# Weight preparation of a recurrent layer: staged W_ih loads, row sums of absolute values on ScalarE, low parts as identity products on TensorE

## The chip, the cores and the metric

One NeuronCore of a Trainium2 chip runs the whole program. The metric is the device time of one execution in microseconds (us). Engine names as in the profile: PE is TensorE (PEld its weight loads), DVE VectorE, ACT ScalarE, POOL GpSimd, SP the engine that only issues transfers here. Each engine works through its own instructions strictly in order. They wait for each other by semaphores.

## The reference

Inputs: x (16 sequences, 256 steps, 512 features) and cond_2048 (16 x 512). Two layers follow each other, each added to its input:

1. Layer 0. Eight block sums of each sequence are scored, weighted and projected to one vector per sequence. It is added to x, and a layer norm follows. Then a feed-forward network (gate, up, down, 512 to 2048 to 512) whose activations and weights are all quantised in blocks of 32. x1 = x + the result.
2. Layer 1. A GRU over the 256 steps with cond_2048 as its first state: gi = x1 W_ih + b_ih and gh = h W_hh + b_hh (each 512 to 1536, cut in thirds r, z, n); r = sigmoid(i_r + h_r), z = sigmoid(i_z + h_z), n = tanh(i_n + r h_n), h' = (1 - z) n + z h. On the states a linear layer with a bias and a mixture of 16 low-rank experts, of which a small router picks two. The output is x1 + the result.

## The kernel before

**Tiles and slots.** The 4096 rows are cut into 32 tiles of 8 time steps times 16 sequences. `over_tiles` (L261) runs a loop of c = -3 to 32, and in each c eight slots s = 0 to 7. It is a software pipeline: at c, the norm and quantisation work on tile c + 4, gate and up on tile c + 3, down and x1 on tile c + 2, the products x1 W_ih on tile c + 1, the recurrence on tile c (one time step per slot, L1283 to L1287 for PE and `recur`, L712, for DVE), and the linear layer with experts on tile c - 1. So the recurrence starts at c = 0. Each engine has a function `slot(c, s)` that issues its instructions in an order written out by hand. There is no planner: an instruction that waits holds up everything behind it on its engine.

**Before the tiles.** `over_pieces` (L273) quantises the feed-forward weights in 24 pieces of 128 x 1024, each going through DVE, POOL, PE (transposes) and ACT (L416 keeps them). Attention and the norm of the first tile run beside the later pieces. c = -3 follows when the last piece is through: PE waits for all 24 kept pieces (L1299).

**High and low parts.** A product of the GRU has nearly fp32 accuracy because each weight and each state is scaled by a power of two and stored as two fp16 numbers, high = fp16(S w) and low = fp16(S w - high). The scale comes from the largest absolute value:

- c = -3, W_hh (loaded into `wih` chunks 0 to 3, each 128 x 1536 fp32). Slot 0: DVE reduces each chunk to a maximum per row (L672), and h as well (L677). PE turns the maxima into a row (`weights_scales`, s = 0, L1272). Slot 1: DVE computes the scales in one partition (`scales_in_row`, L614, L682, L685), and PE spreads them over the partitions (L1277). Slot 2: ACT keeps them (L445, L446). Slots 3 to 6: ACT writes the high part of chunk k (L451), DVE the low part (L699).
- c = -3, slot 6: SP issues the load of the linear layer's weights (`wl`, 1664 KB) and, as the low parts of W_hh are finished, the four chunks of W_ih (768 KB each) into chunks 1 to 4 of the same tile `wih` (L372, L373).
- c = -2, W_ih. Slot 0: DVE reduces its four chunks (L636) and `wl` (L641). Scales as above in slots 0 and 1 (L646 to L652). Slots 3 to 6: high part on ACT (L456), low part on DVE (L658). They are written into the chunk below, so that ACT waits for the low part before.
- c = -1: the first products x1 W_ih (L1151), which need x1T (ACT L502, DVE L903, both in slot 7 of c = -2).
- c = 0: the first state products (L1257) and the parts of `wl`.

**Around it in the same slots**, for the feed-forward tiles f = c + 3 and e = c + 2: PE gate (L1084) in even slots and up (L1090) in odd ones, ACT silu (L475) and DVE the product `inter` (L801) with its quantisation (L762 to L786), POOL qf (L979), PE transposes (L1099) that ACT keeps (L481), and down (L1108). For tile q = c + 4: DVE statistics (L878) and xn (L884, slot 2), POOL times gamma and plus beta (L989, L991). In `slot` of PE the scale products (`weights_scales`) stand ahead of the gate and up products.

Of the kernel before, what the change touches and what calls it, by code (L numbers as in the profile page):

```python
# [24 lines left out]
BF16 = mybir.dt.bfloat16  # L25
# [8 lines left out]
P = 128  # L34
# [28 lines left out]
FILLS = 6  # L63
# [26 lines left out]
def build(nc, x_steps, h0, ident, pick, block_mask, iota, rms_w, query, WkT, WoT, gamma, beta,  # L90
          ffn_w, W_ih, W_hh, b_ih, b_hh, WL, bias, rb1, rw2T, rb2, gates, BT, x1_dram, out):
    with ExitStack() as ctx:
        def sb(name, shape, dt=F32):
            return ctx.enter_context(nc.sbuf_tensor(name, shape, dt))
# [4 lines left out]
        def bank(name):  # L99
# [15 lines left out]
        wih, wl = sb("wih", [P, KD + 1, GATES]), sb("wl", [P, KD + 1, D + ROUTE])  # L115
# [3 lines left out]
        bt = sb("bt", [P, XA // P, D])  # L119
# [51 lines left out]
        x1_in, x1_bias, y = sb("x1_in", [P, D]), sb("x1_bias", [P, D]), sb("y", [P, D])  # L171
# [11 lines left out]
        wst = [sb("wst0", [P, PIECE]), sg_gs[:, 0:PIECE]]  # L183
        qfT_flat = qfT[:, :, :].rearrange("p k n -> p (k n)")
        wy = [gi[:, u * PIECE:(u + 1) * PIECE] for u in range(2)]
        wm = [gi[:, 2 * PIECE:3 * PIECE], sb("wm1", [P, PIECE])[:, :]]
# [18 lines left out]
        chunk_max, most = sb("chunk_max", [P, KD]), sb("most", [P, 2])  # L205
# [15 lines left out]
                             "wl_low_part"))  # L221
        x_small, x_row_ok, x_row_mm, x_scale_mm, x_scale_ok, x_hi = (
# [100 lines left out]
        def _(sp):  # L323
# [61 lines left out]
        def _(act):  # L385
# [54 lines left out]
            def weights(c, s):  # L440

                if c in (-3, -2) and s == 2:
# [5 lines left out]
                if c == -3 and 3 <= s < 3 + KD:  # L448
                    k = s - 3
# [88 lines left out]
        def _(dve):  # L538
# [91 lines left out]
            def input_weights(c, s):  # L630

                at = 2 * KD + 9
                if (c, s) == (-2, 0):
                    for k in range(KD):
                        dve.wait_ge(wih_loaded, 16 * KD)
                        v.tensor_reduce(chunk_max[:, k:k + 1], wih[:, k + 1, :], AX_X, ALU.max,  # L636
                                        apply_absolute_value=True).then_inc(most_dve, 1)
                    dve.wait_ge(most_dve, at)
                    v.reduce_max(most[:, 0:1], chunk_max[:, :], AX_X).then_inc(most_dve, 1)
                    dve.wait_ge(wl_loaded, 16)  # L640
                    v.tensor_reduce(most[:, 1:2], wl[:, 1:KD + 1, :].rearrange("p k n -> p (k n)"), AX_X, ALU.max,  # L641
                                    apply_absolute_value=True).then_inc(most_dve, 1)
# [11 lines left out]
                if c == -2 and 3 <= s < 3 + KD:  # L654
                    k = s - 3
                    dve.wait_ge(scale_kept, 2)
                    dve.wait_ge(wih_hi, k + 1)
                    v.scalar_tensor_tensor(wih_parts[:, k, GATES:2 * GATES], wih[:, k + 1, :], S_I,  # L658
                                           wih_parts[:, k, 0:GATES], ALU.mult, ALU.subtract).then_inc(wih_lo, 1)
# [6 lines left out]
            def gru_weights(s):  # L666


                if s == 0:
                    for k in range(KD):  # L670
                        dve.wait_ge(whh_loaded, 16 * KD)
                        v.tensor_reduce(chunk_max[:, k:k + 1], wih[:, k, :], AX_X, ALU.max,  # L672
                                        apply_absolute_value=True).then_inc(most_dve, 1)
                    dve.wait_ge(most_dve, KD)
                    v.reduce_max(most[:, 0:1], chunk_max[:, :], AX_X).then_inc(most_dve, 1)
# [3 lines left out]
                if s == 1:  # L679
                    dve.wait_ge(most_mm, 1)  # L680
                    scales_in_row(s, KD + 2, least, scale_row)
                    v.tensor_tensor(scale_row[:, 2:3], scale_row[:, 0:1], scale_row[:, 1:2],  # L682
                                    ALU.mult).then_inc(most_dve, 1)
                    dve.wait_ge(most_dve, KD + 8)
                    v.reciprocal(scale_row[:, 3:4], scale_row[:, 2:3]).then_inc(most_dve, 1)  # L685
                if s == 3:
# [9 lines left out]
                if s in (3, 4, 5, 6):  # L696
                    k = s - 3
                    dve.wait_ge(whh_hi, k + 1)
                    v.scalar_tensor_tensor(whh[:, k, 1, :], wih[:, k, :], S_W, whh[:, k, 0, :], ALU.mult,  # L699
                                           ALU.subtract).then_inc(whh_lo, 1)  # L700
# [205 lines left out]
            def slot(c, s):  # L906
# [13 lines left out]
                if c in (-2, 0):  # L920
                    input_weights(c, s)
# [10 lines left out]
        def _(pool):  # L932
            g = nc.gpsimd
            g.memset(minus_half[:, :], -0.5).then_inc(filled, 1)
            g.memset(least_l[:, :], LEAST).then_inc(filled, 1)
# [83 lines left out]
        def _(pe):  # L1019
# [243 lines left out]
            def weights_scales(c, s):  # L1263

                at = (c + 3) * (KD + 9)
                if s == 0:
                    pe.wait_ge(most_dve, at + KD + 2)
# [6 lines left out]
                if s == 1:  # L1274
                    pe.wait_ge(filled, FILLS)
                    pe.wait_ge(most_dve, KD + 9 if c == -3 else 2 * KD + 20)
                    mm(ps_route[:, 0:4], ones_row[:, :], (scale_row if c == -3 else scale_row_l)[:, :], start=True,  # L1277
                       stop=True).then_inc(scale_mm, 1)

            def slot(c, s):  # L1280
# [14 lines left out]
                others(c, s, Q, F, E, I, L)  # L1295

# [60 lines left out]
```

## Time and profile before

| | us |
|---|---|
| median of 3 executions | 1827.99 (1827.65 to 1829.74) |
| the profiled execution, its own time | 1829.66 |
| its span, first to last instruction | 1827.8 |
| PE busy | 1595.1 (87%) |
| DVE busy | 1512.8 (83%) |
| ACT busy | 662.1 (36%) |
| POOL busy | 512.6 (28%) |

The profile is of one execution. Its own time is 1.86 us above its span. Where below the granted clock of TensorE is given, 1.00 is 2.4 GHz and 0.50 is 1.2 GHz; between them both occurred in the stretch. A group of instructions that follow each other is printed as one row with its count. The last duration in a row of matmuls includes the drain of the array. An fp32 matmul of 128 x 512 appears as two records.

### The profile page before, as it was taken

The numbers are of one execution on the slowest core, as the hardware profiler recorded it, in microseconds if no ns is written. First come the engines' busy times: TensorE is split into PE (matmuls) and PEld (weight loads), VectorE is DVE, ScalarE is ACT, GpSimd is POOL, SyncE is SP. The second block draws the span as 40 slices with busy tenths as digits, with TensorE's granted clock in tenths as the row PEclk, the third lists the DMA queues.
The fourth block names the chain that finished last, engine by engine and source line by source line (L and its number), as shares of the span: only waits on it lengthen the run. The fifth ranks groups of instructions, "written<-read, shape, count | busy, mean of one in ns | idle before, by whom it ended". The sixth has DMA issues, their size and how long they took to land.

```text
span 1827.8 us, 76340 instructions
## 1 busy us (share of the span) xinstructions
PE 1595.1 (87%) x32908; PEld 1245.7 (68%) x32908; DVE 1512.8 (83%) x5651; ACT 662.1 (36%) x1712; POOL 512.6 (28%) x572
## 2 busy tenths in 40 slices
PE   5422247999999999999999999999999999999986
PEld 2211114787787778777777777877777777778874
DVE  8999988888888888888888888888888888887654
ACT  1111124444434343443434444344344444344331
POOL 4545423222222222222222222222222222221001
PEclk8755568999999999999999999999999999999997
DMA  6413120000101011000001000001010010000000
GB/s 246 169 63 133 55 92 30 26 15 32 32 32 32 32 32 32 32 32 32 27 31 32 32 32 32 32 32 32 31 32 32 32 32 32 27 19 23 31 15 19
DMA packets 35409, 80.10 MB, mean 44 GB/s; under 512 B 4864, under 2 KB 5248, under 8 KB 34688
## 3 DMA queue, kind: packets, MB, share of 16 engines
q1 hardware_dynamic: 28080, 63.09, 10.1%
q10 hardware_dynamic: 6992, 12.13, 1.9%
q8 instruction: 259, 4.24, 1.0%
q14 instruction: 78, 0.64, 0.1%
HBM read 58.43 MB, written 16.78 MB: 41 GB/s over the span
## 4 chain that ended last, share of the span: by engine, by line
PE 72%; DVE 23%; issue 3%; ACT 1%; DMA 1%; POOL 0%; DVEq 0%; ACTq 0%; SPq 0%; POOLq 0%
PE ps_rn L1257 22%; PE ps_gi L1151 11%; PE ps_z L1257 10%; PE ps_gate_up L1090 6%; PE ps_down L1108 6%; PE ps_base L1160 4%; PE ps_gate_up L1084 4%; PE ps_base L1204 3%; PE ps_route L1160 3%; DVE gi L570 2%; DVE gi L567 2%; DVE wam L544 1%; DVE gi L572 1%; DVE wm L567 1%; DVE fe L769 1%
## 5 line engine op out<-in xcount | busy, mean ns | idle before, releaser
L1257 PE MATMUL ps_rn<-hT,whh 128*128 128x32 f16 x16320 | 449.1, 176 | 37.3 <-DVE hT L707 37.1
L1257 PEld LDWEIGHTS ps_rn<-hT,whh 128*128 128x128 f16 x16320 | 434.9, 96 | 64.0 <-DVE hT L707 58.1
L979 POOL TENSOR_TENSOR qf<-f8c,fe 128x512 bf16<-128x512 bf16 x128 | 135.8, 1061 | 887.1 <-DVE f8c L786 867.6
L1151 PE MATMUL ps_gi<-x1T,wih 128*128 128x128 f16 x4608 | 288.6, 219 | 1.2 <-ACT gi L515 1.2
L1151 PEld LDWEIGHTS ps_gi<-x1T,wih 128*128 128x128 f16 x4608 | 270.3, 98 | 25.6 <-issue 1.5
L524 ACT ACTIVATE r_tanh<-r_pre,scale_half 128x64 f32<-128x64 f32 x256 | 89.0, 348 | 458.3 <-DVE r_pre L727 458.3
L1257 PE MATMUL ps_z<-hT,whh 128*128 128x32 f16 x8160 | 243.2, 176 | 0.0
L1257 PEld LDWEIGHTS ps_z<-hT,whh 128*128 128x128 f16 x8160 | 222.6, 96 | 0.0
L515 ACT ACTIVATE gi<-ps_gi,b_i,scale_x 128x128 f32<-128x128 f32 x384 | 144.7, 457 | 190.7 <-PE ps_gi L1151 190.7
L721 DVE TENSOR_TENSOR r_half<-ps_rn,gi 128x64 f32<-128x64 f32 x256 | 56.6, 221 | 135.4 <-PE ps_rn L1257 135.1
L1084 PE MATMUL ps_gate_up<-wq,qxT 128*128 128x512 bf16 x512 | 134.6, 385 | 14.2 <-DVE inter L801 14.2
L526 ACT ACTIVATE z_tanh<-z_pre,scale_half 128x64 f32<-128x64 f32 x256 | 89.0, 348 | 159.8 <-DVE z_pre L737 159.8
L1090 PE MATMUL ps_gate_up<-wq,qxT 128*128 128x512 bf16 x512 | 137.6, 393 | 2.4 <-ACT sg_gs L475 2.4
L1108 PE MATMUL ps_down<-wq,qfT 128*128 128x512 bf16 x512 | 135.3, 388 | 0.0
L1160 PE MATMUL ps_base<-wl,hT 128*128 128x512 f16 x384 | 96.3, 388 | 0.0
L528 ACT ACTIVATE n<-n_pre,scale_half 128x64 f32<-128x64 f32 x256 | 89.0, 348 | 16.0 <-DVE n_pre L744 5.9
L801 DVE TENSOR_TENSOR inter<-ps_gate_up,sg_gs 128x512 f32<-128x512 f32 x128 | 87.3, 682 | 6.2 <-PE ps_gate_up L1090 6.2
L762 DVE TENSOR_REDUCE fam<-inter 128x16 f32<-128x512 f32 x128 | 87.9, 686 | 4.4
L475 ACT ACTIVATE sg_gs<-ps_gate_up 128x512 f32<-128x512 f32 x128 | 74.2, 580 | 41.7 <-PE ps_gate_up L1084 41.7
L780 DVE SCALAR_TENSOR_TENSOR f<-inter,finv 128x512 fp8e4<-128x512 f32 x128 | 87.6, 684 | 0.0
L1108 PEld LDWEIGHTS ps_down<-wq,qfT 128*128 128x128 bf16 x512 | 48.8, 100 | 50.4 <-issue 5.5
L1090 PEld LDWEIGHTS ps_gate_up<-wq,qxT 128*128 128x128 bf16 x512 | 43.1, 99 | 54.5 <-issue 19.8
(201 smaller groups left out, 2663.6 us busy)
## 6 DMA issues: line engine op xcount, KB each, us to landing
wih<-in_x_steps ACTq DMA_DIRECT2D x32, 256.0 KB, 5.4
xin<-in_x_steps SPq DMA_DIRECT2D x32, 256.0 KB, 3.7
xres<-in_x_steps SPq DMA_DIRECT2D x32, 256.0 KB, 3.3
x_dram<-x SPq DMA_DIRECT2D x32, 256.0 KB, 2.2
x_in<-x_dram SPq DMA_DIRECT2D x32, 256.0 KB, 2.8
out_rows<-y SPq DMA_DIRECT2D x32, 256.0 KB, 2.1
wst<-in_ffn_w SPq DMA_DIRECT2D x12, 512.0 KB, 3.3
sg_gs<-in_ffn_w SPq DMA_DIRECT2D x12, 512.0 KB, 3.6
```

What stands on the lines that cost most here:

```text
L515: last = nc.scalar.activation(gi_gate(i, g)[:, k, :], ps_gi[:, k * P:(k + 1) * P], ACT.Identity, bias=b_i[:, g * KD + k:g * KD + k + 1], s ...
L524: nc.scalar.activation(r_tanh[:, :], r_pre[:, :], ACT.Tanh, scale=HALF_S_INV).then_inc(r_ok, 1)
L526: nc.scalar.activation(z_tanh[:, :], z_pre[:, :], ACT.Tanh, scale=HALF_S_INV).then_inc(z_ok, 1)
L528: nc.scalar.activation(n[:, :], n_pre[:, :], ACT.Tanh, scale=HALF_S_INV).then_inc(n_ok, 1)
L762: v.tensor_reduce(am[:, :], blocked(src[:, :]), AX_X, ALU.max, apply_absolute_value=True).then_inc(small, 1)
L979: g.tensor_tensor(blocked(qf[:, :]), blocked(f8c[:, :]), spread(fe16[:, :]), ALU.mult).then_inc(qf_done, 1)
L1084: last = mm(ps_gate[:, :], qxT[:, k, :], w_ffn(0, n, k), start=k == 0, stop=k == KD - 1)
L1090: last = mm(ps_up[:, :], qxT[:, k, :], w_ffn(8, n, k), start=k == 0, stop=k == KD - 1)
L1108: last = mm(ps_down[:, :], qfT[:, i, :], w_down(i), start=i == 0, stop=i == NF * KD - 1)
L1151: last = mm(ps_gi[:, j * P:(j + 1) * P], wih_parts[:, k, at:at + P], x1T[:, x, k, :], start=k + w + x == 0, stop=k == KD - 1 and w == 1)
L1160: last = mm(out, hT[l % 2][:, 2 * k + x, :], wl_parts[:, k, begin:begin + n], start=k + w + x == 0, stop=stop and w == 1)
L1257: last = mm(ps[:, (at + j) * 2 * B:(at + j + 1) * 2 * B], whh[:, k, u, gate * D + j * P:gate * D + (j + 1) * P], hx(t)[:, 2 * k:2 * k + 2, ...
```

## The change

It touches how the two scales and the two pairs of parts are made at c = -3 and -2, and which memory holds W_ih meanwhile.

1. **Loads.** `wih` has four chunks in place of five. W_ih is loaded into other memory (`wih_staged`: two chunks in `gi`, two in a new tile `stage`, which also holds the buffers of the weight pieces and later `bt`). SP issues the four loads and that of `wl` at (c, s) = (-3, 0), as soon as the last piece has been multiplied by its scale on POOL (`w_out`). `bt` is loaded at (-1, 0), after a wait for all low parts of W_ih.
2. **Scales.** ACT takes, for each chunk and row, the sum of absolute values (`absolute_sums`: Abs with `accum_out`, four for W_hh in slots 0 and 1, four for W_ih in slots 2 to 5, four for `wl` in slot 6, each waiting for the one before). DVE only takes the largest of the four sums. The row of W_hh's maxima on PE moves from slot 0 to 1, DVE's scales from 1 to 2, their spreading on PE to slot 2, ACT's keeping to slot 3. For W_ih DVE takes the largest sums in slot 7 of c = -3; the rest keeps its slots.
3. **Low parts.** DVE's eight instructions go. ACT writes a scaled identity (`scaled_id`, fp32, 128 x 128) once per scale. PE computes S w - high for each chunk as six products into three banks (`low_parts`: per third, an fp32 product with the scaled identity and an fp16 product of the high part with minus the identity), at the end of slots 4 to 7 (c = -3) and 3 to 6 (c = -2). ACT keeps them as fp16 in the following slot (`keep_low`, three instructions), ahead of the next high part. High parts of W_hh move one slot later (4 to 7).
4. POOL writes minus the identity once at the start of the program.

```diff
-        wih, wl = sb("wih", [P, KD + 1, GATES]), ...
+        wih, wl = sb("wih", [P, KD, GATES]), ...
+        stage = sb("stage", [P, 2 * GATES])
+        wih_staged = [x[:, u * GATES:(u + 1) * GATES] for x in (gi, stage) for u in range(2)]
+        scaled_id, minus_id = sb("scaled_id", [P, P]), sb("minus_id", [P, P], F16)
+        ps_low = ps_rn, ps_z, ps_base
...
-                if c == -3 and s == STEPS - 2:
+                if (c, s) == (-3, 0):
+                    sp.wait_ge(w_out, PIECES)
+                    for k in range(KD):
+                        sp.dma_start(wih_staged[k], W_ih[:, k, :]).then_inc(wih_loaded, 16)
                     sp.dma_start(wl[:, 1:KD + 1, :], WL).then_inc(wl_loaded, 16)
-                    for k in range(KD):
-                        sp.wait_ge(whh_lo, min(k + 2, KD))
-                        sp.dma_start(wih[:, k + 1, :], W_ih[:, k, :]).then_inc(wih_loaded, 16)
+                if (c, s) == (-1, 0):
+                    sp.wait_ge(wih_lo, KD)
                     sp.dma_start(bt[:, :, :], BT).then_inc(bt_loaded, 16)
... ScalarE, weights(c, s):
+                def absolute_sums(which, k, w):
+                    wait(act, summed_w, which * KD + k)
+                    nc.scalar.activation(unused[:, 0:w.shape[1]], w, ACT.Abs,
+                                         accum_out=row_sums[:, which, k:k + 1]).then_inc(summed_w, 1)
+
+                def keep_low(k, out, done, more):
+                    act.wait_ge(low_mm, more + k + 1)
+                    for j in range(3):
+                        last = nc.scalar.activation(out[:, j * D:(j + 1) * D], ps_low[j][:, :], ACT.Copy)
+                    last.then_inc(done, 1)
+
+                def identities(scale_of):
+                    wait(act, low_mm, 0 if scale_of is S_W else KD)
+                    nc.scalar.activation(scaled_id[:, :], idf[:, :], ACT.Copy, scale=scale_of).then_inc(low_id, 1)
+
+                if c == -3 and s < 2:
+                    for k in (2 * s, 2 * s + 1):
+                        act.wait_ge(whh_loaded, 16 * KD)
+                        absolute_sums(0, k, wih[:, k, :])
+                if c == -3 and 2 <= s < 2 + KD:
+                    act.wait_ge(wih_loaded, 16 * KD)
+                    absolute_sums(1, s - 2, wih_staged[s - 2])
+                if (c, s) == (-3, 6):
+                    act.wait_ge(wl_loaded, 16)
+                    for k in range(KD):
+                        absolute_sums(2, k, wl[:, k + 1, :])
+                if c == -3 and 5 <= s:
+                    keep_low(s - 5, whh[:, s - 5, 1, :], whh_lo, 0)
+                if (c, s) == (-2, 0):
+                    keep_low(3, whh[:, 3, 1, :], whh_lo, 0)
+                if c == -2 and 4 <= s:
+                    keep_low(s - 4, wih_parts[:, s - 4, GATES:2 * GATES], wih_lo, KD)
... then the scales (slot 3 of c = -3, slot 2 of c = -2) with identities(...), then the high parts:
+                if c == -3 and 4 <= s < 4 + KD:
+                    k = s - 4
                     act.wait_ge(scale_kept, 1)
                     nc.scalar.activation(whh[:, k, 0, :], wih[:, k, :], ACT.Copy, scale=S_W).then_inc(whh_hi, 1)
...
-                    wait(act, wih_lo, k)
-                    nc.scalar.activation(wih_parts[:, k, 0:GATES], wih[:, k + 1, :], ACT.Copy,
+                    act.wait_ge(whh_lo, KD)
+                    nc.scalar.activation(wih_parts[:, k, 0:GATES], wih_staged[k], ACT.Copy,
                                          scale=S_I).then_inc(wih_hi, 1)
... VectorE: the reductions L636, L641, L672 and the low parts L658, L699 are deleted;
+                if s == 1:
+                    dve.wait_ge(summed_w, KD)
+                    v.reduce_max(most[:, 0:1], row_sums[:, 0, :], AX_X).then_inc(most_dve, 1)
... TensorE:
+            def low_parts(k, w, high, high_done, low_done, more):
+
+                pe.wait_ge(high_done, k + 1)
+                pe.wait_ge(low_id, 2 if more else 1)
+                wait(pe, low_done, k)
+                for j, ps in enumerate(ps_low):
+                    mm(ps[:, :], scaled_id[:, :], w[:, j * D:(j + 1) * D], start=True, stop=False)
+                    last = mm(ps[:, :], minus_id[:, :], high[:, j * D:(j + 1) * D], start=False, stop=True)
+                last.then_inc(low_mm, 1)
...
                 others(c, s, Q, F, E, I, L)
+                if c == -3 and 4 <= s:
+                    k = s - 4
+                    low_parts(k, wih[:, k, :], whh[:, k, 0, :], whh_hi, whh_lo, 0)
+                if c == -2 and 3 <= s < 3 + KD:
+                    k = s - 3
+                    low_parts(k, wih_staged[k], wih_parts[:, k, 0:GATES], wih_hi, wih_lo, KD)
```

## Rows read from the trace of the kernel before

**Rows 1.** Stretches (--windows): length, busy PE, PEld, DVE, ACT, POOL, granted clock, DMA, GB/s.
```profile
213.80:250.90 37.10, 18.22 (x66) 7.04 (x66) 33.47 (x58) 12.28 (x15) 13.91 (x11) 0.67 0.36 121
250.90:297.40 46.50, 21.57 (x80) 9.33 (x80) 37.02 (x61) 11.75 (x16) 10.32 (x10) 0.63 0.15 54
600.00:1600.00 1000.00, 987.37 (x21554) 793.19 (x21550) 834.67 (x3558) 406.44 (x1101) 269.21 (x338) 1.00 0.10 32
```
**Rows 2.** The removed DVE instructions: ns min/median/max, first and last start us.
```profile
L672 DVE TENSOR_REDUCE chunk_max<-wih x4: 1741/1742/1744, 213.8 to 218.8; 128x1 f32<-128x1536 f32 x4
L699 DVE SCALAR_TENSOR_TENSOR whh<-wih,scale,whh x4: 1812/1812/1814, 232.9 to 245.0; 128x1536 f16<-128x1536 f32 x4
L636 DVE TENSOR_REDUCE chunk_max<-wih x4: 1742/1743/1752, 253.1 to 258.1; 128x1 f32<-128x1536 f32 x4
L641 DVE TENSOR_REDUCE most<-wl x1: 3609/3609/3609, 259.9 to 259.9; 128x1 f32<-128x3328 f32 x1
L658 DVE SCALAR_TENSOR_TENSOR wih<-wih,scale_l x4: 1796/1916/2222, 276.6 to 289.9; 128x1536 f16<-128x1536 f32 x4
```
**Rows 3.** Timeline where the pieces end, two high parts: start, length us, idle before.
```profile
214.01 1.91 POOL L962 TENSOR_TENSOR qfT<-gi,wsc 128x1024 bf16<-128x1024 f32 x1 [3.15 <-DVE gi L572]
217.11 1.02 ACT L416 ACTIVATE wq<-ps_z 128x1024 bf16<-128x1024 bf16 x1 [3.67 <-PE ps_z L1037]
218.16 1.28 ACT L475 ACT_TABLE_LOAD   x1
220.68 0.21 DVE L677 TENSOR_REDUCE most<-h 128x1 f32<-128x64 f32 x1
...
227.97 3.03 ACT L451 ACTIVATE whh<-wih,scale 128x1536 f16<-128x1536 f32 x2
```
**Rows 4.** ScalarE by line and form: count, busy us, mean ns, idle before.
```profile
L451 ACT ACTIVATE whh<-wih,scale 128x1536 f16<-128x1536 f32 x4 | 6.1, 1569 | 0.0
L438 ACT ACTIVATE proj<-ps_base 128x512 f32<-128x512 f32 x1 | 0.6, 597 | 5.4 <-PE ps_base L1067 5.4
L515 ACT ACTIVATE gi<-ps_gi,b_i,scale_x 128x128 f32<-128x128 f32 x384 | 144.7, 457 | 190.7 <-PE ps_gi L1151 190.7
L432 ACT ACTIVATE acol<-ps_gi 128x1 f32<-128x1 f32 x1 | 0.2, 171 | 7.3 <-PE ps_gi L1058 7.3
```
**Rows 5.** Timeline of TensorE: products of 128x512 and the scale products.
```profile
221.94 1.89 PE L1084 MATMUL ps_gate_up<-wq,qxT 128*128 128x512 bf16 x4
223.76 0.57 PE L1277 MATMUL ps_route<-scale_row,ones_row 1*128 1x4 f32 x2
243.97 1.04 PE L1084 MATMUL ps_gate_up<-wq,qxT 128*128 128x512 bf16 x4 [2.38 <-DVE inter L801]
263.57 1.01 PE L1272 MATMUL ps_route<-idf,most 128*1 128x128 f32 x4 [14.48 <-DVE most L641]
1822.68 1.88 PE L1204 MATMUL ps_base<-bt,wxaT 128*128 128x512 f32 x4
```
**Rows 6.** Timeline of DVE, the first scale row and a slot 2.
```profile
222.04 0.41 DVE L616 TENSOR_REDUCE most_all<-ps_route 1x2 f32<-1x256 f32 x1 [0.34 <-PE ps_route L1272]
223.47 0.15 DVE L685 RECIPROCAL scale_row<-scale_row 1x1 f32<-1x1 f32 x1
271.99 0.54 DVE L884 TENSOR_SCALAR xn<-xs,mv,rstd 128x512 f32<-128x512 f32 x1
272.65 1.26 DVE L771 TENSOR_SCALAR finv<-fe 128x16 uint32<-128x16 uint32 x1
```
**Rows 7.** Timeline of POOL beside them.
```profile
272.61 1.27 POOL L989 TENSOR_TENSOR xg<-xn,gamma_b 128x512 f32<-128x512 f32 x1 [3.63 <-DVE xn L884]
273.96 1.80 POOL L991 TENSOR_TENSOR xg<-xg,beta_b 128x512 f32<-128x512 f32 x1
```
**Rows 8.** Timeline: the end of c = -2 and the first state products.
```profile
296.70 0.75 DVE L903 SCALAR_TENSOR_TENSOR x1T<-ps_turn,scale_x,x1T 128x512 f16<-128x512 f32 x1 [3.67 <-ACT x1T L502]
321.25 1.75 PE L1257 MATMUL ps_rn<-hx_first,whh 128*128 128x32 f16 x64
```

More of the change, by code:

```diff
@@ L62 @@
 LEAST = 2.0 ** -40
-FILLS = 6
+FILLS = 7
 def count(tile, per_tile, more=0):
@@ L110, in build @@
         ps_logit = ps_route[:, ROUTE + P:ROUTE + P + EXPERTS]
[L115 removed]
+        wih, wl = sb("wih", [P, KD, GATES]), sb("wl", [P, KD + 1, D + ROUTE])
         wih_parts, wl_parts = (w[:, :, :].bitcast(F16) for w in (wih, wl))
@@ L118, in build @@
         wq = sb("wq", [P, PIECES, PIECE], BF16)
-        bt = sb("bt", [P, XA // P, D])
+        stage = sb("stage", [P, 2 * GATES])
+        bt = stage[:, 2 * PIECE:3 * PIECE].rearrange("p (m n) -> p m n", m=XA // P)
         proj = sb("proj", [P, D])
@@ L169, in build @@
         hT = [sb(f"hT{u}", [P, 2 * KD, P], F16) for u in range(2)]
-        x1_in, x1_bias, y = sb("x1_in", [P, D]), sb("x1_bias", [P, D]), sb("y", [P, D])
+        x1_in_bias, y = sb("x1_in_bias", [P, 2 * D]), sb("y", [P, D])
+        x1_in, x1_bias = x1_in_bias[:, 0:D], x1_in_bias[:, D:2 * D]
         xa = sb("xa", [P, ROUTE])
@@ L180, in build @@
         wxaT = sb("wxaT", [P, XA // P, P])
-        wst = [sb("wst0", [P, PIECE]), sg_gs[:, 0:PIECE]]
+        wst = [stage[:, 0:PIECE], sg_gs[:, 0:PIECE]]
+        wih_staged = [x[:, u * GATES:(u + 1) * GATES] for x in (gi, stage) for u in range(2)]
         qfT_flat = qfT[:, :, :].rearrange("p k n -> p (k n)")
         wy = [gi[:, u * PIECE:(u + 1) * PIECE] for u in range(2)]
-        wm = [gi[:, 2 * PIECE:3 * PIECE], sb("wm1", [P, PIECE])[:, :]]
+        wm = [gi[:, 2 * PIECE:3 * PIECE], stage[:, PIECE:2 * PIECE]]
         wqn = [qfT_flat[:, u * PIECE:(u + 1) * PIECE] for u in range(2)]
@@ L203, in build @@
         acol = sb("acol", [P, 1])
-        chunk_max, most = sb("chunk_max", [P, KD]), sb("most", [P, 2])
+        row_sums, most = sb("row_sums", [P, 3, KD]), sb("most", [P, 2])
+        unused = x1_in_bias[:, :].bitcast(BF16)
+        scaled_id, minus_id = sb("scaled_id", [P, P]), sb("minus_id", [P, P], F16)
+        ps_low = ps_rn, ps_z, ps_base
         most_all, least, power, inverse = (sb(x, [1, 2]) for x in ("most_all", "least", "power", "inverse"))
@@ L221, in build @@
                              "wl_low_part"))
+        summed_w, low_id, low_mm = sem("weight_row_sums"), sem("scaled_identity"), sem("low_part_sums")
         x_small, x_row_ok, x_row_mm, x_scale_mm, x_scale_ok, x_hi = (
@@ L440, in weights @@
             def weights(c, s):
-                if c in (-3, -2) and s == 2:
+                def absolute_sums(which, k, w):
[27 more added lines that the diff above has]
+                    keep_low(s - 4, wih_parts[:, s - 4, GATES:2 * GATES], wih_lo, KD)
+                if (c, s) in ((-3, 3), (-2, 2)):
                     act.wait_ge(scale_mm, c + 4)
@@ L447, in weights @@
                                          ACT.Copy).then_inc(scale_kept, 1)
-                if c == -3 and 3 <= s < 3 + KD:
-                    k = s - 3
+                    act.wait_ge(scale_kept, c + 4)
+                    identities(S_W if c == -3 else S_I)
+                if c == -3 and 4 <= s < 4 + KD:
+                    k = s - 4
                     act.wait_ge(scale_kept, 1)
@@ L630, in input_weights @@
             def input_weights(c, s):
[L632 to L642, printed above, removed]
+                at = 9
+                if (c, s) == (-3, 7):
+                    dve.wait_ge(most_mm, 1)
+                    dve.wait_ge(summed_w, 3 * KD)
+                    for i in range(2):
+                        v.reduce_max(most[:, i:i + 1], row_sums[:, i + 1, :], AX_X).then_inc(most_dve, 1)
                 if (c, s) == (-2, 1):
@@ L653, in input_weights @@
                         .then_inc(most_dve, 1)
[L654 to L659, printed above, removed]
                 if c == 0 and s < KD:
@@ L666, in gru_weights @@
             def gru_weights(s):
[L669 to L675, printed above, removed]
+                if s == 1:
+                    dve.wait_ge(summed_w, KD)
+                    v.reduce_max(most[:, 0:1], row_sums[:, 0, :], AX_X).then_inc(most_dve, 1)
                     dve.wait_ge(h0_loaded, 16)
@@ L919, in slot @@
                     gru_weights(s)
-                if c in (-2, 0):
+                if c in (-3, -2, 0):
                     input_weights(c, s)
@@ L934, in _ @@
             g.memset(minus_half[:, :], -0.5).then_inc(filled, 1)
+            pool.wait_ge(first_consts, 32)
+            g.tensor_scalar(minus_id[:, :], idf[:, :], -1.0, None, ALU.mult).then_inc(filled, 1)
             g.memset(least_l[:, :], LEAST).then_inc(filled, 1)
@@ L1263, in weights_scales @@
             def weights_scales(c, s):
-                at = (c + 3) * (KD + 9)
-                if s == 0:
-                    pe.wait_ge(most_dve, at + KD + 2)
+                if s == (1 if c == -3 else 0):
+                    pe.wait_ge(most_dve, 2 if c == -3 else 11)
                     pe.wait_ge(q_ev, c + 4)
```

17 lines of the change are left out of this document (6 added, 11 removed).

## Prediction

> **What bounds the kernel now.** I began with the busy time by stretches. From 600 to 1600 us PE is busy 987 of 1000 us at the full clock [rows 1]: the steady part, with the recurrence in it, is PE's. The change puts no instruction there, so it can only move the moment at which the recurrence starts. Everything it touches lies between 213.8 us, where DVE ends the last weight piece, and 321.25 us, where the first state product starts [rows 8]. In that stretch DVE is busy 33.5 of 37.1 us and then 37.0 of 46.5 us, PE under half, ACT 12.3 and 11.8 us [rows 1]. The chain of waits runs through DVE there, with its reductions and low parts as the largest pieces [rows 2]. A reader should see two things: DVE is the bound of this stretch, and PE's clock is only 0.67 and 0.63 in it [rows 1], so PE work put there is not priced at its steady rate.
>
> **What goes.** DVE loses 4 x 1.74 + 4 x 1.81 + 4 x 1.74 + 3.61 + 7.85 (four L658, 1.80 to 2.22) = 32.7 us [rows 2]. If all of it were on the path and all that replaces it were hidden, that is the most the change can give.
>
> **What comes, per instruction.** *Row sum of a 128 x 1536 chunk (ACT).* The same shape as a high part takes 1.57 us [rows 4]. The trace has no accumulating ACT instruction. Below: 1.4 us (immediate scale in place of one from memory might save a little). Above: 2.1 us, if the accumulator's read is an instruction with a drain of its own (0.5 us, the size of a 128 x 128 one, L515). I take 1.57 + 0.17, a one-column instruction (L432) = 1.75 us; each waits for the one before, so no overlap. For `wl` (832 columns) by length 0.85, 0.1 of fixed cost and 0.17: some 1.15 us. In all 8 x 1.75 + 4 x 1.15 = 18.6 us on ACT.
> *Low part of a chunk (PE).* Two fp32 products of 128 x 512 at the full clock take 1.88 us with a drain of some 0.17, so 0.855 each; four 16-bit ones take 1.04 us with it, so 0.216 each, and 1.89 at half clock, 0.43 each [rows 5]. Three of both: 3.2 us at the full clock, 6.4 at half (the fp32 product doubled).
> *Keeping it (ACT).* Three instructions of 128 x 512 from PSUM at 0.60 [rows 4], and neighbours overlap (two of 1.57 took 3.03 [rows 3]): 1.6 us, at most 1.8. *Identity*: 128 x 128, 0.3 us of 0.46 (L515, which has a bias and scale from memory) and 0.17 (L432), twice only.
> *POOL's minus identity* lies at the start, where POOL has no other work before the first piece's scales: 0, and some 0.4 us if that cover were gone.
> *Loads.* 3.1 + 1.7 MB are issued at 216 instead of around 240 us. ACT asks for W_ih after 227 us and for `wl` after 250 us, so neither is waited for. If they were 5 us late, ACT would wait inside the time in which it waits for a gate product anyway (step B). In SP's queue they pass only the loads of xin, whose data the next c needs. The wait ahead of `bt` is for low parts that end a slot earlier: 0.
>
> **The walk on the new path.** Times from the span's start; 0.05 to 0.2 us per handover is included.
> *A.* POOL ends the last piece at 215.9, PE and ACT keep it by 218.1 [rows 3]. Before, DVE did its reductions beside that. Now ACT can only begin then, as the sums stand behind L416: two sums 3.5, the table load 1.3, silu 0.6, two sums 3.5: 227.1. DVE's two small reductions: 227.7, against 220.9 [rows 3]. +6.8.
> *B.* On PE the row of maxima (0.9) is now ahead of up (slot 1): 228.6, then up at half clock 1.9: 230.5. DVE's scales now stand in slot 2 behind inter, its reduction and xn: 0.7 + 0.7 + 0.54: 232.4. xn releases POOL's two instructions of 1.27 and 1.80 us [rows 7], and small DVE instructions wait while POOL works (L771, 16 columns wide, took 1.26 us and ended with L989, at 273.9 [rows 6, 7]). So the scale row, 1.6 us by itself (222.04 to 223.6 [rows 6]), ends at 236.6, against 223.6. +13.
> *C.* Behind it on PE stands the second gate. Spread 0.5, gate 1.9, silu 0.6: 239.7. ACT holds its sums of slots 3 and 4 behind this silu: sum 1.75, scales kept 0.25, identity 0.3, sum 1.75, first high part 1.57: 245.4.
> *D.* From here PE and ACT alternate. Low part k+1 waits for high part k+1, which stands on ACT behind keeping low part k, which waits for PE. A round is low 3.2 + 0.2 + keep 1.6 + high 1.6 = 6.6 us at the full clock, and nothing in it overlaps. Low 0 begins at the half clock: 5.4. Round 0: 245.5 to 254.3. Low 1 (3.2) ends at 257.5, but ACT has the four sums of `wl` first, until 259.1; keep and high: 262.2. Low 2, after 5 us with little on PE, mostly at half: 6.2; keep, high: 271.8. Low 3: 275.0. The scale row of W_ih on PE stands behind it: 275.9, against 264.6 (L1272, 263.57 + 1.01 [rows 5]). +11.3.
> *E.* c = -2: scales on DVE 2.4, spread 0.5, up, gate, silu, a transpose kept: first high part ends at 284.4. Three rounds of 6.6 and a last low part 3.2: 307.6. Keep 1.6, then scale_x 0.2, and both parts of x1T 0.7 each: 311.0, against 297.45 (296.70 + 0.75 [rows 8]). +13.5. DVE, the old bound, idles in this stage.
> *F.* c = -1 is unchanged, and the steady part hands on the whole shift.
>
> The other end of D and E is PE at the full clock from the first low part on. It takes 5.2 us from low 0 and low 2, and some 1.5 from the gates between: +7. I take **+12 us**, nearer to the walk. The profiled execution's own time of 1829.66 would become 1841.7. The median shown is 1827.99, 1.7 below it, so the forecast for the median is **1840.0 us**.
>
> On the clock: four gate products took 1.89 us at 221.94 and 1.04 us at 243.97 [rows 5], so both levels occur in this stretch. The Trainium skill ("TensorE: Matmul & The Clock Gate", The HAM clock gate) says that a PE which has been busy for a while is given the full 2.4 GHz. By that rule, if the identity products keep PE busy enough, the clock end of +7 would hold and the time would be 1835; the rows alone leave it open, as no stretch with such products is in the trace.
>
> **The rivals.**
> *R1, hidden: faster.* The eight rounds of D and E are so short that DVE's missing 32.7 us count. Place: PE's low parts. The walk is 12 us too long over eight low parts, so it turns once a low part takes less than 3.2 - 12/8 = 1.7 us, that is if an fp32 product with an identity costs about 0.35 us instead of 0.855. At the 16-bit price, 0.216 [rows 5], a low part takes 1.3 us: 8 x 1.9 = 15.2 us less, -3 us: 1825. For it: PE is half idle here [rows 1]. Against it: fp32 products of this shape have one price in rows 5, and the order of D is in the code. Chance 0.07.
> *R2, ACT switches tables.* One table load of 1.28 us stands between the copies and the silu [rows 3]. If Abs needed another table than silu, slots 1 to 6 of c = -3 would switch six times more: 6 x 1.3 = 8 us on ACT, most of it on the path: +20, 1848. For it: there is no Abs in the trace. Chance 0.05. The Trainium skill ("ScalarE: Activation LUTs", Table sets) says that abs stands in every table set as filler; by this rule there is no switch.
> *R3, PE stays at half clock* (0.50) through all low parts: 6.4 instead of 3.2 for six of them, 19 us more: +31, 1859. Against it: the clock did rise at 243.97 with less work on PE. Chance 0.05.
> *R4, no change.* The sums and low parts slip into slots in which PE and ACT wait for DVE, and the scale row of step B is not held up: D begins at 236 rather than 245, and with the full clock the gain in E falls away: +7 - 9 = -2 to +2. It needs both. Chance 0.08.
>
> **How the numbers follow.** Forecast 0.75, R1 0.07, R2 0.05, R3 0.05, R4 0.08. Own range of the forecast: +7 less 1 to +17 (sums of 2.1 us put 0.35 x 8 = 3 to 5 us on it), 1834 to 1846. To leave out no more than 2 in 10, it reaches to 1832 and to 1849, with R2 inside. What this measurement can tell from no change is about 0.2%, 3.7 us. Faster: R1 in part and a tail of R4, 0.07. Same: R4 and the rest of R1, 0.07. Slower: 0.86.
>
> **What would show it.** In the profile after: DVE at well under 60% between 214 and 310 us; the last of W_hh's four sums ending at about 227; the scale row ending near 236 with a long small instruction beside POOL's L991; four rounds of 6.6 us in c = -2, in which keep waits for PE and PE for the high part; x1T's low part near 311 and the first state product near 334; the rest of the trace the same, shifted. It is wrong if the low parts take under 2 us, if DVE's small instructions aren't held up, if PE's low part of chunk k+1 runs beside the keeping of chunk k, or if the steady part returns some of the shift.

## Result and profile after

| | before | after |
|---|---|---|
| median | 1827.90 us (1827.65 to 1829.74, 4 executions) | 1841.46 us (1838.82 to 1842.77, 4 executions) |
| the profiled execution, its own time | 1829.66 | 1842.34 |
| its span | 1827.8 | 1840.5 |
| start of the first state product | 321.25 | 329.83 |
| PE / DVE / ACT busy | 1595.1 / 1512.8 / 662.1 | 1620.5 / 1479.1 / 690.1 |

After over before is 1.0067, 95% interval 1.0055 to 1.0079: slower by 13.6 us between the medians. The forecast was 1840.0, from a median before of 1827.99. In a second measurement (`after_again` below) the change had 1839.87 us against 1829.25 us for the kernel before on the same chip: 10.6 us, 1.0056 (1.0042 to 1.0070).

Three stretches of the kernel after, with the columns of [rows 1]: the building of W_hh, that of W_ih, and a piece of the steady part:

```profile
213.80:250.90 37.10, 18.59 (x57) 7.03 (x58) 15.64 (x44) 22.30 (x32) 9.66 (x9) 0.59 0.37 145
250.90:297.40 46.50, 37.86 (x136) 16.13 (x134) 20.82 (x57) 24.43 (x42) 10.31 (x10) 0.93 0.06 17
600.00:1600.00 1000.00, 987.17 (x21539) 792.93 (x21538) 833.88 (x3557) 406.92 (x1103) 271.79 (x343) 1.00 0.09 31
```

DVE, the old bound, fell from 33.5 to 15.6 us and from 37.0 to 20.8 us of busy time [rows 1]. No engine took its place at 100%: ACT is busy 60% and then 53%, PE 50% and 81%. The stretch became longer because the two wait for each other, which busy shares alone don't say. Four rows from the list of waits of the kernel after, from 213.8 to 306 us, say it (engine, line, awaited engine and line: us in total, times, longest):

```profile
DVE inter L824 <- PE ps_gate_up L1115: 25.1, 6, 8.8
ACT wih L459 <- PE ps_base L1311: 14.1, 4, 4.3
ACT whh L459 <- PE ps_base L1311: 9.0, 3, 4.3
DVE most L703 <- ACT x_in_bias L453: 8.3, 1, 8.3
```

L459 keeps the low parts, L1311 is the last product of one: ACT stood 23.1 us waiting for them. DVE stood 25.1 us for up products. Three of these six waits, of 2.57, 8.80 and 5.64 us, are for up products that stand on PE behind a low part, 17.0 us together; the other three are not.

**Steps A and B** in the timeline of the kernel after (start, length, instruction, idle before):

```profile
217.87 1.48 ACT L453 ACTIVATE x_in_bias<-wih 128x1536 bf16<-128x1536 f32 x1
219.24 0.19 ACT L453 ACTIVATION_READ_ACCUMULATOR x_in_bias<-wih 128x1 f32 x1
...
226.25 0.21 DVE L705 TENSOR_REDUCE most<-h 128x1 f32<-128x64 f32 x1
...
232.74 1.26 POOL L1016 TENSOR_TENSOR xg<-xg,beta_b 128x512 f32<-128x512 f32 x1
233.12 0.90 DVE L662 TENSOR_SCALAR power<-most_all 1x2 uint32<-1x2 uint32 x1
...
234.80 0.15 DVE L713 RECIPROCAL scale_row<-scale_row 1x1 f32<-1x1 f32 x1
```

The accumulator's read is an instruction of its own, 0.19 us, and a sum takes 1.66 us from start to start (217.87 to 219.53). L705 ends at 226.5, where its predecessor ended at 220.9 [rows 3]. The scale row ends at 234.95, 11.3 us later than before [rows 6]; L662, two elements wide, took 0.90 us and ended with POOL's L1016.

**Step E**, low parts 0 and 1 of W_ih in the timeline of PE, and the same ones' keeping on ACT below:

```profile
277.76 1.12 PE L1310 MATMUL ps_rn<-gi,scaled_id 128*128 128x512 f32 x2
...
280.88 0.38 PE L1311 MATMUL ps_base<-wih,minus_id 128*128 128x512 f16 x1
...
284.38 1.46 PE L1310 MATMUL ps_rn<-gi,scaled_id 128*128 128x512 f32 x2 [2.04 <-ACT wih L499]
285.63 0.63 PE L1311 MATMUL ps_rn<-wih,minus_id 128*128 128x512 f16 x1
286.06 1.91 PE L1310 MATMUL ps_z<-gi,scaled_id 128*128 128x512 f32 x2
```

```profile
281.29 0.60 ACT L459 ACTIVATE wih<-ps_rn 128x512 f16<-128x512 f32 x1 [3.58 <-PE ps_base L1311]
281.79 0.59 ACT L459 ACTIVATE wih<-ps_z 128x512 f16<-128x512 f32 x1
282.26 0.60 ACT L459 ACTIVATE wih<-ps_base 128x512 f16<-128x512 f32 x1
282.74 1.59 ACT L499 ACTIVATE wih<-gi,scale_l 128x1536 f16<-128x1536 f32 x1
```

Here is one round: low part 277.76 to 281.3, kept by 282.9, high part 282.74 to 284.3, next low part 284.38. It is 6.62 us, and every piece stands behind another. The second low part ran in part at 1.2 GHz (an fp32 product and its drain 1.91 us in place of 1.02), and its round took 8.31 us. PE had idled 2.04 us before it. But it idled as long before the fourth low part, at 299.30, and that one ran at the full clock (1.02), so the idle time just before doesn't decide it by itself.

### The profile page after: what moved, and what is told of

Same layout as the page of the kernel before. It is cut to its first block, busy times and chain, and to the rows that moved or that the text cites. A ratio compares the mean times of both kernels' runs of the same rounds, so it can differ in the third digit from the quotient of the medians.

```text
span 1840.5 us, 76535 instructions
## 1 busy us (share of the span) xinstructions
PE 1620.5 (88%) x32980; PEld 1256.5 (68%) x32980; DVE 1479.1 (80%) x5635; ACT 690.1 (37%) x1762; POOL 510.9 (28%) x573
## 4 chain that ended last, share of the span: by engine, by line
PE 74%; DVE 20%; ACT 3%; issue 2%; POOL 0%; DMA 0%; DVEq 0%; ACTq 0%; POOLq 0%
PE ps_rn L1282 22%; PE ps_gi L1176 11%; PE ps_z L1282 10%; PE ps_gate_up L1115 6%; PE ps_down L1133 6%; PE ps_base L1185 4%; PE ps_gate_up L1109 4%; PE ps_base L1229 3%; PE ps_route L1185 3%; DVE gi L613 2%; DVE gi L610 1%; DVE wam L587 1%; DVE gi L615 1%; DVE stage L610 1%; DVE fe L792 1%
## 5 line engine op out<-in xcount | busy, mean ns | idle before, releaser
L1133 PE MATMUL ps_down<-wq,qfT 128*128 128x512 bf16 x512 | 132.9, 382 | 0.0
L1133 PEld LDWEIGHTS ps_down<-wq,qfT 128*128 128x128 bf16 x512 | 48.2, 99 | 48.4 <-issue 2.1
```

The lines of the kernel that those rows point to most:

```text
L1133: last = mm(ps_down[:, :], qfT[:, i, :], w_down(i), start=i == 0, stop=i == NF * KD - 1)
```

## Experiments

Each is built from the change except `before_delayed`, and each was timed beside the kernel before on the same chip. The median of the kernel before lies between 1828.72 and 1829.25 us in all of them. A ratio is that to the kernel before. The start of the first state product is read from one profile each; two profiles of one program differ there by 0.1 us (the change) and 0.6 us (`sums_beside`).

### Which part costs: two parts, on and off

**staged_only.** Part 1 alone.

```diff
- absolute_sums, keep_low, identities (ScalarE), low_parts (TensorE)
+ v.tensor_reduce(row_sums[:, 1, k:k + 1], wih_staged[k], AX_X, ALU.max, ...)      # (-2, 0), as L636
+ v.scalar_tensor_tensor(whh[:, k, 1, :], ...); the same for wih_parts             # slots 3 to 6, as L699, L658
```

> Part 1 of the change alone: W_ih goes to the other memory and is loaded from 216 us on; maxima and low parts stay on DVE in the slots of before. All theories: DVE no longer waits 2.4 us for the last chunk of W_ih and ACT's high parts of W_ih no longer wait for the low part of the chunk below. DVE stays the bound, so 2 to 4 us less: first state product at 317 to 319 us (before 321.25, after 329.83), time 1824 to 1826.

Measured: first state product at 319.63 us, 1.6 us earlier. Time 1828.61 against 1828.86, ratio 0.9996 (0.9987 to 1.0005): no change. The expectation of 2 to 4 us was too high. DVE no longer waits 2.42 us for W_ih, but it takes the maxima only 1.67 us earlier (251.40 in place of 253.07): an up product before them took 1.89 us in place of 1.04, at the lower clock, and the product `inter` behind it came 0.84 us later. That ACT's high parts of W_ih no longer wait brought nothing more: DVE's last low part starts 1.61 us earlier (288.25 in place of 289.86).

**maxima_dve.** The change without part 2.

```diff
- absolute_sums(...)                                       # ScalarE
+ v.tensor_reduce(row_sums[:, 0, k:k + 1], wih[:, k, :], AX_X, ALU.max, ...)       # slot 0; W_ih and wl at (-2, 0)
- if s == (1 if c == -3 else 0):
+ if s == 0:                                               # the scale row one slot earlier, high parts in 3 to 6
```

> The change with part 2 undone: DVE takes the maxima as before, the scales of W_hh are made in slots 0 to 2, low parts stay on PE and ACT (W_hh one slot earlier than in the change). Theory T1 (the alternation of PE and ACT for the low parts is the cost): rounds of 6.6 us stay, and DVE's reductions of W_ih (10.3 us) come behind them, so little is won: first state product 327 to 332, time 1838 to 1843. Rival T2 (the late sums and scale row of steps A and B are the cost): first high part 13 us earlier and most of it kept, first state product near 320, time 1828 to 1832.

Measured: first high part at 229.57 (change: 241.50), yet the first state product at 333.89, 4.1 us later than in the change and 1.9 us later than T1 allowed. Time 1841.57, 1.0061 (1.0048 to 1.0075). T2 fell: the 12 us won at the first high part were lost again before the recurrence.

**low_dve.** The change without part 3.

```diff
- keep_low(...), identities(...)                           # ScalarE
- low_parts(...)                                           # TensorE
+ v.scalar_tensor_tensor(whh[:, k, 1, :], wih[:, k, :], S_W, whh[:, k, 0, :], ALU.mult, ALU.subtract)
```

> The change with part 3 undone: sums on ACT as in the change, low parts on DVE again (W_hh in slots 4 to 7, W_ih in 3 to 6). T1: the late scale row costs 13.5 us at the first high part, but DVE's reductions (17 us) are gone and the slots after it run at DVE's pace of about 4.5 us; first state product 318 to 322, time 1826 to 1831, 10 to 14 below the change. T2: the delay of steps A to C stays in full: first state product near 329, time 1837 to 1842.

Measured: first state product at 315.10, time 1824.85, ratio 0.9978 (0.9969 to 0.9987): faster than before. T2 fell. T1 had the direction, but the gain was larger than it gave: both numbers lie below its ranges.

The starts of the first state product, as a table:

| us | low parts on DVE | low parts on PE and ACT | difference |
|---|---|---|---|
| maxima on DVE | 319.63 (staged_only) | 333.89 (maxima_dve) | +14.3 |
| sums on ACT | 315.10 (low_dve) | 329.83 (the change) | +14.7 |
| difference | -4.5 | -4.1 | |

By this measure the two parts hardly touch each other. The sums, with the slots that move with them, start the recurrence 4 us earlier even where they stand, behind the last piece. The low parts cost 14 to 15 us. The median times say the same of the low parts (1828.61 to 1841.57, and 1824.85 to 1839.87 or 1841.46). For the sums they show 3.8 us beside DVE's low parts (1828.61 to 1824.85), but beside PE's no clear gain: 1.0061 without them, 1.0067 and 1.0056 with them. So their 4 us are shown at the start of the recurrence in both rows, and in the time only in one.

### Alternation or volume

**high_first.** The change with two statements turned round on ACT.

```diff
+ high part of chunk k
  keep_low(k - 1)
- high part of chunk k
```

> The change with one thing turned round on ACT: the high part of chunk k+1 is written before the low part of chunk k is kept. T1: the round loses the high part, 6.6 to 5.0 us; three rounds in c = -2 and about two in c = -3 count: 6 to 9 us less than the change, first state product 321 to 324, time 1832 to 1836. Rival T3 (it is the volume of PE's products and their clock, not the alternation): less than 2 us less, time 1839 to 1842.

Measured: first state product at 320.56, 9.3 us earlier than the change. Time 1829.32, ratio 1.0011 (1.0002 to 1.0020), 1832 to 1836 expected. The spread is wider than that of the kernel before (1827.2 to 1831.0): six of the eleven executions took 1828.8 to 1829.3 us, the other five 1831.8 to 1835.0. The profile is of one of the six, so what the five did is open. The same products run on PE. Low parts 2 and 3 of W_ih in its timeline:

```profile
284.91 1.04 PE L1310 MATMUL ps_rn<-stage,scaled_id 128*128 128x512 f32 x2
...
287.94 0.38 PE L1311 MATMUL ps_base<-wih,minus_id 128*128 128x512 f16 x1
...
290.07 1.10 PE L1310 MATMUL ps_rn<-stage,scaled_id 128*128 128x512 f32 x2 [0.67 <-ACT wih L459]
```

The round is 5.16 us in place of 6.62, and PE waits 0.67 us. T3 (volume and clock) fell as the main cause. Part of the gain is the clock: it was 1.00 from 250.9 to 297.4 us, where the change had 0.93:

```profile
250.90:297.40 46.50, 39.73 (x162) 17.70 (x160) 23.18 (x62) 29.96 (x49) 12.57 (x12) 1.00 0.08 23
```

In c = -2 the sizes can be told apart. From the first low part to the last it is 15.7 us (274.39 to 290.07), in the change 21.5 (277.76 to 299.30). Of these 5.9 us the round at the lower clock makes up 1.7 (8.31 in place of 6.62) and the order the rest. That the clock follows from the shorter waits is a reading of two profiles; no run set the clock by itself. And the order doesn't take back the whole cost: with all low parts on DVE (`low_dve`) the first state product came at 315.10, 5.5 us earlier still.

### The scale row (step B)

**row_early.** The change with one call moved.

```diff
+                if (c, s) == (-3, 2):
+                    gru_weights(s)
                 beside(0)
...
-                if c == -3:
+                if c == -3 and s != 2:
                     gru_weights(s)
```

> The change with DVE's scale row of W_hh put ahead of the slot's other DVE work in slot 2 of c = -3. Step B says that it ended at 234.95 us because inter, its reduction, xn and POOL's L1016 came first; here it can end near 229.3, the second gate product starts 5.4 us earlier (230.2 in place of 235.6) and everything behind follows: first state product 324 to 325 us (change 329.83), time 1834 to 1837. Rival: the row is held up by something else or the rounds of PE and ACT take the time up; less than 2 us of gain.

Measured: the scale row's first instruction starts at 227.81 in place of 232.69, and L662 behind it takes 0.16 us in place of 0.90; the first high part starts at 235.51 (change: 241.50), the first state product at 325.32, 4.5 us earlier. Time 1835.90, 1.0037 (1.0023 to 1.0051), against 1839.87 for the change on the same chip. Step B is real: put ahead, the row takes 4.5 of the 8.6 us away. It ends 5.6 us earlier (229.34 in place of 234.95), and most of that is its place in DVE's queue. POOL's part in the change is 1.8 us: L794 took 1.25 us beside L1014 and L662 0.90 us beside L1016, while alone they take 0.17 and 0.16 us in `row_early`.

```profile
227.81 0.41 DVE L659 TENSOR_REDUCE most_all<-ps_route 1x2 f32<-1x256 f32 x1 [1.11 <-PE ps_route L1298]
228.26 0.16 DVE L662 TENSOR_SCALAR power<-most_all 1x2 uint32<-1x2 uint32 x1
```

### Behind the first state product

**before_delayed.** The kernel before, with more work for DVE ahead of its maxima.

```diff
                 if s == 0:
+                    for k in range(5):
+                        v.tensor_reduce(spare[:, k:k + 1], wih[:, k % KD, :], AX_X, ALU.max, ...)
```

> The kernel before with five more DVE reductions of a W_hh chunk (8.4 us, results unused) ahead of its maxima: the start of the recurrence is moved by as much as in the change (8.6 us) and nothing else differs. It tells where the rest of the change's 13.5 us is from (its part behind the first state product took 1510.7 us in the profiled execution, 1506.5 before). C1: the part behind the first state product does not depend on when it starts: 1837 plus or minus 1. C2: a later start costs some us more there, as in the change: 1840 to 1842.

Measured: first state product at 328.53 (7.3 us later, 8.6 expected), time 1838.26 against 1829.25: 9.0 us, between the two expectations. Behind the first product the profiled execution took 1836.3 - 328.5 = 1507.8 us.

**after_again.** The change, unaltered.

> The changed kernel once more, for more executions and another profile. C1 or chance in TensorE's clock: the executions spread over 1838 to 1843, and a profiled one near 1839 has a part behind the first state product of about 1507 us, with fewer stretches at 1.2 GHz after 400 us than the first one had. C2: it is 1510 us again with the same stretches.

Measured: 1839.87 (1838.97 to 1840.59); the profile has the first product at 329.71 and 1838.8 - 329.7 = 1509.1 us behind it. The first profile had 1510.7. The granted clock is where they differ. First profile of the change, then the second (same columns as above):

```profile
1290.00:1300.00 10.00, 9.07 (x154) 6.45 (x151) 8.49 (x34) 2.86 (x8) 1.61 (x2) 0.83 0.01 2
1700.00:1840.50 140.50, 114.89 (x2751) 93.11 (x2748) 79.84 (x393) 41.24 (x121) 11.76 (x25) 0.88 0.08 23
```

```profile
1290.00:1300.00 10.00, 9.07 (x207) 7.62 (x206) 8.52 (x34) 3.79 (x11) 1.50 (x2) 1.00 0.01 2
1700.00:1838.80 138.80, 112.82 (x2718) 91.29 (x2714) 79.13 (x392) 40.53 (x120) 11.72 (x25) 0.91 0.07 21
```

In the first, PE fell to 1.2 GHz for some 3 us inside the steady part, behind a gap of 0.93 us that both have. What it cost can be read from the state products around it, first profile above, second below:

```profile
1293.07 1.76 PE L1282 MATMUL ps_rn<-hT,whh 128*128 128x32 f16 x64 [0.93 <-DVE hT L730]
1300.50 1.75 PE L1282 MATMUL ps_rn<-hT,whh 128*128 128x32 f16 x64
```

```profile
1292.96 1.76 PE L1282 MATMUL ps_rn<-hT,whh 128*128 128x32 f16 x64 [0.93 <-DVE hT L730]
1298.87 1.75 PE L1282 MATMUL ps_rn<-hT,whh 128*128 128x32 f16 x64
```

Up to there the two agree to 0.01 us: 963.24 and 963.25 us from the first state product. The next product comes 7.43 us later in the first and 5.91 us later in the second, so the fall of the clock cost 1.5 us, and that is nearly all of their difference of 1.6. That PE stood at 1.2 GHz for longer in the first one's tail cost at most 0.1 us: from the product at 1700.72 (1699.13 in the second) to the end both take 139.7 to 139.8 us.

The same products divide the difference to the kernel before (1506.5 us). It has 962.29 us up to the first of them, 0.95 less than the change, 0.7 of which is there 48 us behind the first state product. Its tail takes 138.0 us, 1.7 less. But the tail has 139.5 us in `before_delayed` and 139.6 in `staged_only`, whose recurrence starts earlier than before, so the longer tail doesn't belong to the change. What sets it is open.

The thirteen profiles behind this text have 1506.4 to 1510.7 us behind the first product, whatever the start: 1506.4 with the maxima on DVE (first product at 333.89), 1509.0 in sums_beside (309.54). So C1 holds within the spread of single executions; a fixed extra cost of about 1 us for a later start (before_delayed: 9.0 for 7.3) is neither shown nor excluded.

### A better division

**sums_beside.** Staged loads; the sums of W_ih and `wl` on ACT, behind the other work of their slots; W_hh's maxima and all low parts on DVE.

```diff
                 others(c, s, Q, F, E, I, L)
+                if c == -3:
+                    sums_beside(s)     # W_ih chunk s - 2 in slots 2 to 5, wl in slot 6
```

> Staged loads, DVE maxima of W_hh in slot 0 as before, ACT sums for W_ih and wl only, each behind its slot's other ACT work in c = -3, low parts on DVE. T1 and step A: ACT's sums lie in time in which ACT waited, DVE loses 10.3 us of reductions on the path, nothing alternates: 10 us less than staged_only (first state product 319.63): 309 to 312 us, time 1817 to 1820. Rival (sums hold ACT up in c = -3 whatever their place): 313 or later, time over 1822.

Measured: first state product at 309.54, time 1820.27, ratio 0.9946 (0.9933 to 0.9960).

**sums_beside_2.** The same, beside the next two.

> The same kernel as sums_beside, beside the two above on one chip: 1818 to 1821, within 1 us of its first median relative to the kernel before.

Measured: 1818.85, ratio 0.9948 (0.9935 to 0.9962), first product at 308.99. What the expectation calls the two above are `sums_early` and `half_low`, which follow here.

**sums_early.** W_hh's sums too, before the last two pieces.

```diff
+                if (c, s) == (-4, 6):
+                    act.wait_ge(whh_loaded, 16 * KD)
+                    for k in range(KD):
+                        absolute_sums(0, k, wih[:, k, :])
```

> sums_beside with the sums of W_hh on ACT too, but ahead of the last two weight pieces (slot 6 of c = -4), where ACT waits from 201.2 to 211.5 us: four sums are 6.7 us. Step A said that the sums cost because they come behind the last piece; there they cost nothing and DVE loses its 6.7 us of maxima. The row of maxima on PE stands behind the last transposes and the wait for all kept pieces (218.0), so it can come 2.8 us earlier only (220.9 before); DVE has the rest as slack. First state product 303 to 307 (sums_beside 309.54), time 3 to 6 us below sums_beside. Rival: the last piece's path bounds the slots behind, and less than 2 us is won.

Measured: **1814.63 us** (1812.96 to 1815.32) against 1828.72, ratio 0.9922 (0.9909 to 0.9936); first state product at 306.45. It beats both kernels, and `sums_beside` (measured again as `sums_beside_2`, on the same chip) by 4.2 us. Its first and its last sum on ACT, and the keeping of the two pieces that follow:

```profile
201.17 1.48 ACT L451 ACTIVATE x_in_bias<-wih 128x1536 bf16<-128x1536 f32 x1
...
205.99 1.48 ACT L451 ACTIVATE x_in_bias<-wih 128x1536 bf16<-128x1536 f32 x1
...
211.57 0.60 ACT L540 ACTIVATE qxT<-ps_route 128x512 bf16<-128x512 bf16 x1 [4.00 <-PE ps_route L1172]
212.42 1.02 ACT L425 ACTIVATE wq<-ps_gate_up 128x1024 bf16<-128x1024 bf16 x1 [0.26 <-PE ps_gate_up L1070]
217.12 1.02 ACT L425 ACTIVATE wq<-ps_z 128x1024 bf16<-128x1024 bf16 x1 [3.68 <-PE ps_z L1070]
```

ACT still waits 4 us for PE before L540, so the four sums delay nothing, and the last piece is kept at the same time as before (217.11 [rows 3]).

**half_low.** sums_early with low parts 1 and 3 of each matrix on PE and ACT.

```diff
+                if c in (-3, -2) and s in (4, 6):      # TensorE, k = s - 3
+                    low_parts(...)
+                if c in (-3, -2) and s in (5, 7):      # ScalarE, behind the high part
+                    keep_low(...)
```

> sums_early with the low parts of chunks 1 and 3 of both matrices on PE and ACT, those of 0 and 2 on DVE: no two parts of PE follow each other, and ACT writes the next high part before it keeps the low part. T1 (alternation, not PE's volume): DVE loses 7.5 us, PE's parts stand ahead of the next gate or up product and give some back: 0 to 4 us below sums_early. T3 (any low part on PE delays gate and up, 3.2 to 6.4 us each): up to 6 us above it.

Measured: 1814.67, ratio 0.9927 (0.9914 to 0.9941), first product at 306.10: no gain over sums_early (1814.63). That is the border between the ranges of T1 and T3, so the run doesn't decide between them. DVE lacks four low parts, 7.2 us in sums_early, and waits instead. PE's low part 1 of W_hh is 5.0 us in the way of the next up product (L1133):

```profile
234.75 2.02 PE L1328 MATMUL ps_rn<-wih,scaled_id 128*128 128x512 f32 x2
...
239.54 0.38 PE L1329 MATMUL ps_base<-whh,minus_id 128*128 128x512 f16 x1
239.76 1.03 PE L1133 MATMUL ps_gate_up<-wq,qxT 128*128 128x512 bf16 x4
```

DVE's `inter` behind that up product starts at 240.89, in sums_early at 240.66: the low part that DVE no longer makes has won nothing there. So a low part on PE has two prices: the round with ACT, and the gate and up products behind it. The second was not measured alone.

## Why the prediction was right, step by step

The sign, the mechanism and the size of the time were right: 1840.0 forecast, 1841.46 and 1839.87 measured. But that the size is so close is luck: the chain was 3.4 us shorter than forecast (8.6 for 12), and in the profiled execution 4.1 us came behind it that no term of the sum had.

- **A.** Forecast 227.7 for DVE's small reductions, measured 226.5. A sum was 1.66 us in place of 1.75.
- **B.** Forecast 236.6, measured 234.95. POOL held DVE up as L771 had shown [rows 6, 7]; POOL's second instruction took 1.26 us, not 1.80. Without POOL the row would still have come late, behind `inter`, its reduction and xn (`row_early`).
- **C.** Forecast 245.4 for the end of the first high part, measured 243.1 (L494, 241.50 + 1.56).
- **D.** Forecast 29.6 us for four rounds, measured 25.7 (from 243.1 to the start of the row of maxima at 268.77, which ends at 269.4). PE left its half clock earlier: low 0 took 4.0 us in place of 5.4, low 2 5.2 in place of 6.2. And the sums of `wl` held up the keeping of low 1 by 0.4 us (253.7 to 254.1) in place of 1.6. The forecast for the row, 275.9, was 6.5 us late with its parts from A to D.
- **E.** Forecast 35.1 us from there to x1T's low part at 311.0, measured 36.7 us from the row's end at 269.4 to 306.0 (305.28 + 0.75). Three rounds were 6.6 us each in the forecast. They were 6.62, 8.31 and 6.61: the low part in the middle one ran in part at half clock, which I had expected in D and not here. The chain to this point is 8.6 us longer than before, where I had 13.5 in the walk and took 12.
- **F.** From x1T to the first state product it is 23.8 us before and after [rows 8], as forecast.
- **What failed** is the clause that the steady part hands on the whole shift and adds nothing. It did hand on 8.6 us. But behind the first product the profiled execution took 4.1 us more than before, the same program's second one 2.5 us and the delayed kernel 1.2 us. Of the 4.1 us, 1.5 are the fall of the clock at 1295 us, which the second profile doesn't have, and 1.7 a longer tail, which kernels without the change have too. The remaining 0.9 stand near the start of the recurrence in both profiles of the change; their cause is open. The prediction took no account of this spread of single executions, and its range was wide enough to hold it.
- **The rivals.** R1 needed a low part under 1.7 us; it was 3.3 at the full clock (277.76 to 281.09). R2 did not come: there is one table load in the stretch, as before. The rule quoted from the Trainium skill ("ScalarE: Activation LUTs", Table sets), that abs stands in every set, agrees with this trace: Abs and silu alternate with the one load at 221.13. R4 did not come: the scale row was held up, and D began at 243.1. R3 did not come: the clock was 0.93 from 250.9 to 297.4 us, where [rows 1] had 0.63. The rule of the clock gate that the prediction quotes from the Trainium skill ("TensorE: Matmul & The Clock Gate", The HAM clock gate) agrees with this in its direction. The 1835 that went with it did not come. The chain was 8.6 us longer where that end had 7, with 1.7 us of it in the one round in c = -2 that ran in part at half clock; the rest of the way to 1841.46 stands behind the first state product.
- **Loads.** W_ih and `wl` were there in time; no wait of ACT for a transfer is in the list of waits.

## What to carry to other kernels

When work leaves the busiest engine for two idle ones, write down the chain through both before adding up busy time: high part, product, keeping were 6.6 us a round in series, where DVE's low parts of W_ih before followed each other every 4.3 to 4.8 us with all its other work between them (276.6 to 289.9 [rows 2]). The order inside one engine's queue can halve such a cost (here 9 us for two statements turned round), and work that needs no partner, as the row sums, is free where its engine already waits (`sums_early`): move that, and leave the rest. And weigh a result near 0.2% against the same program run twice, since TensorE's clock may drop in one execution and not in the next, 1.5 us here.

## What the hardware showed that I had not expected

- POOL's L1016 takes 1.26 us where DVE waited for it (the L662 above), and L991, the same instruction in the kernel before, 1.80 where DVE ran beside it [rows 7].
- PE lost its full clock inside a part in which it is busy 98.7%: 0.83 over the 10 us from 1290 in one execution, 1.00 in another of the same program, with the same gap of 0.93 us before.
- A scalar sum costs an extra instruction of 0.19 us for the accumulator, though it follows its activation without a gap; the sum and the read together are barely longer than the 1.57 us of a scaled copy, whose scale comes from memory.
